# Expert pairs of a fused two-layer kernel: product and silu first in the slot, result scaling and turned copy last, seven row transfers moved under pairs 0 to 2

## What is computed

```python
def _L1_ffn_ref(hidden_states, W_A, W_B, W_up, W_down):
    E, K, H, F, R = (8, 2, 128, 256, 64)
    gate_hidden = jnp.einsum('nh,erh->ner', x, W_A)
    scores = jnp.sqrt(jnp.sum(gate_hidden * gate_hidden, axis=-1))
    topk_scores, topk_idx = jax.lax.top_k(scores, K)
    topk_w = jax.nn.softmax(topk_scores, axis=-1)
    ...
    g = jnp.einsum('ner,efr->nef', gate_hidden, W_B)
    up = jnp.einsum('nh,efh->nef', x, W_up)
    y = jnp.einsum('nef,ehf->neh', jax.nn.silu(g) * up, W_down)
    out = jnp.einsum('neh,ne->nh', y, w_full)

x = x + _L1_attn_ref(xn, ...) + _L1_ffn_ref(xn, ...)
```

## Time and profile before

| | us |
|---|---|
| median of 3 runs | 655.79 |
| lowest and highest | 652.28 to 659.21 |
| the profiled execution | 649.94 |
| its span, first to last instruction | 648.1 |

### The profile page before, as it was taken

How to read it: one execution, slowest core, us unless ns; L and a number is a source line. 1 busy time by engine, 2 the same in 40 slices (tenths; PEclk the granted TensorE clock), 3 DMA queues, 4 the chain that set the end, 5 groups by cost and what they waited for, 6 DMA issues and landing times.

```text
span 648.1 us, 10568 instructions
## 1 busy us (share of the span) xinstructions
PE 567.0 (87%) x3218; PEld 467.6 (72%) x3218; DVE 447.0 (69%) x1199; ACT 300.8 (46%) x558; POOL 298.2 (46%) x268
## 2 busy tenths in 40 slices
PE   5899999989899998999999999986877877888870
PEld 2879985667687677888888878765665666777660
DVE  6858998729721992344659989987787685656673
ACT  4460247655424441344577657855835433334230
POOL 5610030006561563265334458768344755666661
PEclk9999999999999998999999999997999799999995
DMA  7350031400023502133222232122211232322626
GB/s 215 128 243 17 2 129 33 97 9 2 21 110 110 172 0 65 59 93 94 75 67 79 70 100 79 39 99 68 56 55 59 59 89 71 82 73 67 208 74 223
DMA packets 48381, 54.94 MB, mean 85 GB/s; under 512 B 7029, under 2 KB 40374, under 8 KB 47271
## 3 DMA queue, kind: packets, MB, share of 16 engines
q1 hardware_dynamic: 43542, 42.99, 21.2%
q0 software_dynamic: 4320, 8.99, 4.1%
q10 hardware_dynamic: 466, 2.31, 1.6%
HBM read 36.22 MB, written 15.94 MB: 80 GB/s over the span
## 4 chain that ended last, share of the span: by engine, by line
PE 30%; DVE 12%; issue 9%; ACT 6%; POOL 4%; another core or an unknown queue 4%; DMA 2%; SPq 1%; POOLq 0%; ACTq 0%; DVEq 0%
PE banks L1762 4%; PE banks L1764 4%; PE banks L1763 4%; PE banks L1968 3%; PE banks L1882 2%; PE banks L2119 2%; PE banks L1874 2%; POOL arena L888 1%; PE banks L2104 1%; PE banks L1895 1%; PE banks L1896 1%; DVE arena L1606 1%; DMA arena<-result_rows 1%; PE banks L2075 1%
## 5 line engine op out<-in xcount | busy, mean ns | idle before, releaser
L873 POOL DMA_INDIRECT result_rows<-arena x71 | 69.3, 975 | 38.8 <-PE banks L1764 16.6
L858 POOL DMA_INDIRECT expert_rows<-arena x64 | 63.6, 994 | 40.6 <-issue 14.6
L822 POOL TENSOR_TENSOR arena<-arena 128x512 f32<-128x512 f32 x32 | 40.8, 1275 | 86.2 <-DVE arena L1431 86.2
L888 POOL TENSOR_TENSOR arena<-arena 128x512 f32<-128x512 f32 x32 | 42.4, 1325 | 68.2 <-DVE arena L1585 68.1
L1585 DVE TENSOR_TENSOR arena<-banks,arena 128x512 f32<-128x512 f32 x48 | 33.0, 688 | 42.5 <-PE banks L1764 33.5
L1968 PEld LDWEIGHTS banks<-arena 128*128 128x128 f32 x384 | 48.8, 191 | 6.9 <-POOL arena L888 3.0
L1968 PE MATMUL banks<-arena 128*128 128x128 f32 x384 | 51.6, 277 | 1.9 <-DVE arena L1585 1.1
L1874 PE MATMUL banks<-arena 128*128 128x512 f32 x96 | 50.5, 608 | 2.4 <-DVE arena L1431 1.1
L1882 PEld LDWEIGHTS banks<-arena 128*128 128x128 f32 x256 | 33.0, 191 | 19.0 <-POOL arena L822 14.4
L2119 PE MATMUL banks<-arena 128*128 x284 | 39.6, 284 | 7.4 <-DVE arena L1628 4.0
L1087 ACT ACTIVATE rows_hi<-banks 128x256 fp32r<-128x256 f32 (+1 forms) x36 | 13.6, 379 | 67.7 <-remote 33.6
(11 more groups left out here) (281 smaller groups left out, 1628.7 us busy)
## 6 DMA issues: line engine op xcount, KB each, us to landing
arena<-expert_weights SPq DMA_DIRECT2D x64, 128.0 KB, 3.4
arena<-expert_rows SPq DMA_DIRECT2D x71, 66.0 KB
arena<-in_x SPq DMA_DIRECT2D x8, 512.0 KB, 6.8
arena<-result_rows SPq DMA_DIRECT2D x8, 512.0 KB
arena<-in_dft_f SPq DMA_DIRECT2D x1, 2048.0 KB, 9.6
normed_hi<-xnt_hi SPq DMA_DIRECT2D x1, 2048.0 KB, 6.4
normed_lo<-xnt_lo SPq DMA_DIRECT2D x1, 2048.0 KB, 10.9
arena<-in_dft_i SPq DMA_DIRECT2D x1, 2048.0 KB, 7.7
```

The source lines that it names most:

```text
L822: nc.gpsimd.tensor_tensor(out=T1[:, q % 3, :], in0=T1[:, q % 3, :], in1=T2[:, q % 2, :], op=ALU.add).then_inc(y_in, 1)
L858: pool.indirect_dma_start(out=xrows, out_offset=bass.IndirectOffsetOnAxis(ap=SLOT[:, k, t:t + 1], axis=0), in_=XNF[:, t, :], in_offset=Non ...
L873: pool.indirect_dma_start(out=yrows, out_offset=bass.IndirectOffsetOnAxis(ap=DEST[:, i, n:n + 1], axis=0), in_=YB[:, i % YBUFS, n, :], in_ ...
L888: nc.gpsimd.tensor_tensor(out=AM0[slot % 2], in0=AM0[slot % 2], in1=WB0[:, m, :], op=ALU.mult).then_inc(weighted, 1)
```

## The change

Three things are done. On DVE `product(i)` moves directly behind `rows_lo(i + 1)`, and `result_rows(i - 2)` to the end of the slot. On ACT `silu_pair(i)` moves directly behind `rows_hi(i + 1)`, and `turned(i - 1)` to the end. On POOL the second quarter sends 9 transfers in slots 43 to 48 and its last seven under pairs 0, 1 and 2 (3, 3, 1); the waits on the routing matmul go away; the third quarter starts with pair 4 instead of pair 3, and two results go out under pair 3.

```diff
-SCATTER_FROM = (33, 43, 54, 64)
-ROWS_FROM = 55
+SCATTER_FROM = (33, 43, 56, 64)
+ROWS_FROM = PAIR0
-SCATTERS = ((1, 3, 3, 1, 1, 2, 1, 1, 3), (1, 1, 1, 3, 3, 2, 2, 2, 1))
+SCATTERS = ((1, 3, 3, 1, 1, 2, 1, 1, 3), (1, 2, 2, 2, 1, 1))
...
-            rows, results, of_slot = 2 * BT * 2, 0, {}
+            rows, results, of_slot = sum(map(sum, SCATTERS)), 0, {}
...
-                known = 2 * BT * (3 if slot < SCATTER_FROM[3] else 4)
+                known = 2 * BT * sum(slot >= first for first in SCATTER_FROM)
...
-                        if N0 * NCH < slot < PAIR0:
-                            pool.wait_ge(gh_mm, TPC * (NCH - 2) + slot - N0 * NCH)
                         scatter(shares_of[slot - first])
```

In ACT's loop:

```diff
                     rows_hi(i + 1)
+                if 0 <= i < NP:
+                    silu_pair(i)
...
                         attention_copy(n)
-                if 0 <= i < NP:
-                    silu_pair(i)
-                if 1 <= i <= NP:
-                    turned(i - 1)
                 c = due(slot, 13)
...
+                if 1 <= i <= NP:
+                    turned(i - 1)
```

In DVE's loop:

```diff
                     rows_lo(i + 1)
+                if 0 <= i < NP:
+                    product(i)
...
                 if 0 <= i < NP:
-                    product(i)
                     places_of(i)
-                if 2 <= i < NP + 2:
-                    result_rows(i - 2)
...
                             tables(bt, part)
+                if 2 <= i < NP + 2:
+                    result_rows(i - 2)
```

## The result

Beside the kernel before on the same chip (654.03 us, median of 4 runs, 648.18 to 659.21), the changed kernel took 665.71 us (661.84 to 666.14): ratio 1.020, interval 1.015 to 1.025. So it is slower, by 11.7 us between the medians. Repeated beside other runs of the kernel before it came out slower each time, by different amounts: 1.011 (1.007 to 1.015) and 1.030 (1.022 to 1.038). The experiments found two kinds of chips behind a part of that spread. Ratios leave out a few executions that ran over 1.5% above the fastest of their kernel, so they can differ a little from those of the medians.

What follows compares the result with a forecast made beforehand. TensorE was taken to set the pace, with about 15 us idle under the later pairs. Terms 8.6 + 0.6 - 2.3 - 2.4 - 0.8 + 5.6 - 1.0 + 0.5 = +8.8 us gave 664.5 us, range 656 to 674.

Steps and rivals of the forecast that it cites:

- Pair 4's rows: TensorE's turn of pair 4's rows waits for the moved transfers: 468.8 instead of 459.32, leaving product 4 8.6 us late.
- two side effects: Low part behind pair 2's product, pair 0's turned copy behind the exponential: up to 2 us each, hidden under pair 4's wait.
- The clock: TensorE falls to half clock after pair 4's wait, slowing pair 3's gate and up: +0.6 us, bounds 0 and 1.3.
- Results last, pairs 3 to 11: Under pairs 3 to 11, later work fills idle time on DVE (-2.3 us) and ACT (-2.4), with -0.8 for the clock.
- the -0.8: TensorE's clock may stay up before the matmuls at 504.49: half of up to 1.5 us gained.
- the -2.3: DVE's idle time before pair 2's results is filled with key sums and tables, gaining 2.3 us.
- Results later: Pair 16's slot sends three rows and two results on POOL, delaying results: +0.5 us, bounds 0 and 1.3.
- The attention drain: DVE's drain behind the product makes TensorE wait 0.7 us in each of 16 slots: +5.6 us, bounds 0 and 11.2.
- the pauses only take up TensorE's lead: Rival: attention drains cost nothing, as pauses only remove the lateness of TensorE's signals; +3.2 us, 659, chance 0.24.
- Nothing before pair 0: Transfer changes in slots 44, 45 and 49 to 51 cost zero, since POOL had idle time there.
- The listed signs: Trace signs: pair 4's turn 8 to 10 us behind pair 3's, SP waiting 10 us more, longer drain waits, shorter product waits.
- The fourth rival: Faster: TensorE's late signals go away, ACT and DVE start up to 3 us earlier in 11 slots; 642.6 at 22 us, chance 0.10.

Runs made afterwards that it cites:

- second pair of traces: Traces of the two unchanged kernels, the one before and the changed one, on another chip; spans 650.7 and 658.3 us.
- b3_order_drain_first: Against the kernel before: new order on ACT and DVE, but attention drain ahead of the product; transfers as before. 655.99 us, ratio 1.004.
- a2_order: Against the kernel before: all the change's order edits on ACT and DVE, transfers as before. 646.86 us, ratio 1.028.
- c2_swap: Against the kernel before: only DVE's product and attention drain exchanged. 641.47 us, ratio 1.018.
- a4_last: Against the kernel before: only turned copy (ACT) and result scaling (DVE) moved last in the slot. 629.75 us, ratio 0.997.
- c0_after: The changed kernel, unchanged, run again on a chip where the kernel before takes 631.7 us. 653.75 us, ratio 1.030.
- a1_transfers: Against the kernel before: only the seven row transfers moved under pairs 0 to 2, order on ACT and DVE as before. 639.97 us, ratio 1.016.
- c1_three: Against the kernel before: three row transfers instead of seven moved, into pair 0's slot; order and third quarter's start as before. 630.82 us, ratio 1.001.
- b2_drain_first: The changed kernel with DVE's attention drain ahead of the product again. 658.99 us, ratio to the kernel before 1.007.
- b0_before: The kernel before, unchanged, run for a trace from the same chip as its neighbours. 652.62 us.
- d1_low_first: b3_order_drain_first with pair 2's product on DVE moved behind the last key bias and low part. 632.35 us, ratio 0.999 to the kernel before.

## Why the prediction was right, and where its terms were not

The forecast said slower, about 8.8 us by the sum; the medians say 11.7, and 7 on the second chip of this kind. The sum was made of terms of which some were good and some were not. By stretches it booked 0 up to pair 1's turn, +9.5 to pair 4's, -5.8 to pair 12's and +5.1 behind it. Measured were -2.9, +9.5, -1.4 and +8.2 in the first pair of traces and -3.0, +9.3, +0.3 and +4.4 in the second. The direction and the largest term are earned; that the total comes near is in part luck, since a saving before pair 1 that nobody foresaw stands against savings and costs that were mis-sized.

**Pair 4's rows: right, by two errors.** Predicted 468.8, measured 468.69. The two moments can be compared only because pair 1's turn happens to stand at the same place in both traces (446.79 and 446.68). The last transfer started at 462.43 instead of 461.5, since the root started at 450.23 instead of 449.04 (the first transfer at 453.57 instead of 452.2), and from it to the turn took 6.3 us instead of 7.3; that the two cancel is luck. The wait was not on the DMA all along. Half of the hole lay before `down_rows(0)`, the side effect that the text named and hid under the cover. Its two side effects were put at "up to 2 us" each without the cover. Together they are 4.2 (pair 1 to 4 in b3_order_drain_first against before; 3.4 from pair 0's turn, and 2.7 to 3.0 on the prompt chips, a2_order against c2_swap and a4_last), because the low part is now also behind the table load and silu. Under the cover they cost nothing: c0_after and a1_transfers both take 21.9.

**The clock: too small.** Product 3 was to start 7.6 + 0.6 late (7.5 + 0.6 by the prediction's own 471.2) and was 8.9 late (472.61 against 463.69); product 4, to be 8.6 + 0.6 late, was 9.9. From the turn of pair 4's rows to silu 3 it had been 1.80 us (459.32 to 461.12). Now silu began 0.63 before product 3, at 471.98, that is 3.29 behind the turn. So the half clock cost 1.5 instead of my 0.6, beyond my upper bound of 1.3. The granted clock was 0.58 over the hole and 0.72 over the 6.8 us behind it (0.50 up to 471.9, 0.93 after). The Trainium skill (TensorE: Matmul & The Clock Gate, The HAM clock gate) says that an idle TensorE falls back to half its clock; the term by that rule was 1.3, and this trace, with 1.5, agrees with it.

**Results last, pairs 3 to 11: the pieces right, the sum not.** Pair 5's slot: product 4 was 9.9 late and product 5 7.5, so -2.4 (predicted -2.3). ACT's idle time before pair 8's turned copy is gone, and `rows_hi(11)` came at 507.56 instead of 501.34, 6.2 late, where the turn of pair 10's rows before it was 8.7 late: -2.5 (predicted -2.4). The clock did not stay up, though: the first matmul of pair 11's gate and up still took 0.78 us:

```profile
511.37 0.78 PE L1761 MATMUL banks<-gate_up_weights_hi,rows_hi 128*128 x1
```

So the -0.8 was nothing. And the -2.3 did not reach TensorE in full: from pair 4's to pair 12's turn only 1.4 us came back, and none in the second pair of traces, where 5.8 were booked (8.6 - 9.5 + 0.6 - 2.3 - 2.4 - 0.8). What takes their place is the turned copy, last on ACT. TensorE's waits between the two turns, changed kernel:

```profile
PE banks L2103 <- ACT arena L1099: 2.3, 2, 1.6
PE banks L2118 <- ACT arena L1099: 2.2, 2, 1.3
```

That is 4.5 us, and 8.0 in the second trace of the changed kernel; the traces of the kernel before have none between these turns; the waits for products (2.4 us in 4) are gone in return. Behind pair 12 TensorE also waits more for the result scaling (6.0 us in 4 and 10.3 in 6, against 3.0 and 3.2 in 3 before). The prediction booked the late copy with its own 0.6 us and no wait of TensorE for it. That a4_last gained nothing says the same.

**Results later: there, and larger.** The term was +0.5, bounds 0 and 1.3. From pair 17 to 20 the changed kernel took 1.6 and 0.7 us more, a1_transfers 1.9 more than a4_last and c1_three; the rows of a1_transfers above show the wait for the buffer.

**The attention drain: the size near on this kind of chip, the mechanism only half.** From pair 12 on, +8.2 and +4.4 us in the two pairs of traces, against the +5.1 of my last terms. But the working took pair 20's slot, in which silu was already over when DVE could begin, and so arrived at 0.7 a drain. Where signals are prompt this does not hold: the drain then waits for gate and up as well, and so does L1659, which the working left out. TensorE waits 1.4 us for each of 12, and the exchange of product and drain costs 10 to 12 us (c2_swap). My bound of 11.2 covered that by accident. Where signals are late, the undoing of that exchange gave nothing (b2_drain_first). So on this kind of chip the rival "the pauses only take up TensorE's lead" describes the drains better than my middle value, and the increase under pairs 17 to 34 of the changed kernel is not traced to one cause. TensorE's waits for the drain were 5.0 us in 4 in the changed kernel (the rows of waits above), with 9.9 in 8 more on L2144 and L2138 put down to "issue"; before it was 5.1 in 4, with 5.7 in 4 more put down to "issue". Both together grew from 10.8 to 14.9, and from 10.3 to 14.1 in the second pair of traces: 4 us, where c2_swap has 13 more than c1_three. What the runs suggest is: a pause costs its length where TensorE is followed promptly, and little where its signals are late anyway. The second half rests on b2_drain_first alone; neither the swap nor the new order was run by itself on a chip with late signals.

**Nothing before pair 0: wrong.** Slots 43 to 51 were booked at zero. Up to pair 1's turn the changed kernel took 2.9 and 3.0 us less on chips with late signals. It is not spread over these slots: up to pair 0's turn it took 0.7 and 0.6 us more, and from pair 0's turn to pair 1's 3.8 us instead of 7.5. ACT and TensorE there, before:

```profile
444.42 0.38 ACT L1087 ACTIVATE rows_hi<-banks 128x256 fp32r<-128x256 f32 x1 [4.79 <-remote]
...
445.35 0.80 PE L1762 MATMUL banks<-router_weights_hi,normed_hi 128*128 128x512 f32 x1 [4.31 <-ACT arena L1068]
```

Pair 0's rows had been turned at 439.32, for 0.38 us. ACT took them up 4.7 us after that; ACT's square for the routing (L1068) stood behind it, and TensorE waited for the square and then ran at half clock. In the changed kernel ACT took them up 0.42 us after the start of the turn. This one late signal is in all three traces with the transfers in their old places on such a chip (before, b0_before, b3_order_drain_first: 6.7 to 7.5 us from turn to turn) and in none of the three with the transfers moved (3.8). On the prompt chips it is 3.8 us wherever the transfers stand, so there was nothing to be gained, and that is one reason why the ratio is worse there. SP was slow in the same place: before, six loads took 11.86 us while POOL's transfers were running, in the changed kernel eight took 8.10. TensorE did not wait for these loads.

**The listed signs.** True: the DMA-ended wait at pair 4, and ACT without idle time before pair 8's copy. True only if it is counted against the trace before: pair 4's turn is 9.4 us later than there, but 12.8 behind pair 3's, where "8 to 10" stood; before, that distance was 5.1 already. True but larger: SP's wait for the quarter grew by 16.5 us instead of 10, since it also starts earlier. In part: waits for the drain L1648, as above; those for products fell from 4.6 us in 7 to 0.4 in 1. Of ACT's late signals 9.0 us in 4 times ("remote") and 12.5 in 6 ("issue") are left of 33.6 in 11 and 6.7 in 4:

```profile
ACT rows_hi L1085 <- PE banks L2074: 52.2, 18, 8.9
...
ACT rows_hi L1085 <- issue: 12.5, 6, 3.1
...
ACT rows_hi L1085 <- remote: 9.0, 4, 3.0
```

So 40.3 us became 21.5; in the second pair of traces 34.2 became 28.2, of which pair 0's late signal alone is 4.8. The fourth rival was not without ground, since a part of that lateness did vanish; but the slots from pair 12 on did not become shorter for it.

## What to carry to other kernels

An engine's instruction that waits for a long chain should not stand ahead of one that is ready, even if both are short: where signals are prompt, the drain cost TensorE 3.4 us of waits as long as it filled DVE's wait for silu, and 10 us more time once it stood behind it. When transfers are moved under later work, count from the start of the last one to the first user, and look for what else has silently moved behind the same cover; two costs in one hole are paid once, and removing the smaller alone shows nothing (pair 1 to 4 took 21.9 us with both and 21.9 with the transfers alone). A difference of one or two per cent should be measured on more than one chip before it is believed as a number.

## What the runs showed of the hardware

Chips differ in how promptly TensorE's signals reach the others, or occasions do: each group of runs had one chip on one occasion, so the two can't be told apart. The same kernel before took 654.0 and 653.3 us on two occasions and 629.6 and 631.7 on two others. In all six traces of the first kind ACT waited before `rows_hi` for signals that came well behind the matmul's record, in sum 9 to 34 us in 4 to 11 times by the waits put down to "remote" (21 to 40 us in 10 to 15 times with those put down to "issue"), up to 4.8 us at once. In the eight traces of the other kind nothing is put down to "remote", and ACT began `rows_hi` right behind the turn's record in every slot from pair 13 on.

On the first kind several of SP's register and load instructions took 0.70 to 0.72 us each while POOL's indirect transfers followed each other closely (439 to 445 us before). With the same transfers running on a prompt chip (a2_order, a4_last) they took 0.02 to 0.39. Whether both have one cause was not tried, and neither was what in the chips differs. The changed kernel cost +1.1 and +2.0% on the one kind and +3.0% on the other. The first two differ as much as the last two, and the intervals of +2.0 and +3.0 overlap, so the kind of chip explains only a part of that spread. Plainer is the drain's place: worth 10 us or more on prompt chips (c2_swap; a2_order against d1_low_first), nothing measurable on the other (b2_drain_first).
